# A transformer block with adaptive norms: who rounds the first norm's output, when attention maxima are transposed, and where score blocks stand

## The reference, cut to what matters

```python
c6 = silu(c) @ Wc + bc
sh_msa, sc_msa, g_msa, sh_mlp, sc_mlp, g_mlp = split(c6, 6)
xm = ln(x) * (1 + sc_msa) + sh_msa                     # first norm
q, k, v = xm @ Wq + bq, xm @ Wk + bk, xm @ Wv + bv     # 16 heads of 16 features
w = softmax(q @ k.T / 16)
x = x + g_msa * ((w @ v) @ Wo + bo)
xm2 = ln(x) * (1 + sc_mlp) + sh_mlp                    # second norm
x = x + g_mlp * (gelu(xm2 @ W1 + b1) @ W2 + b2)
```

## Time and profile before

| | before |
|---|---|
| median of 3 runs | 710.11 us (709.73 to 710.66) |
| the profiled execution | 708.81 us |
| its span, first to last instruction | 707.0 us |
| mean granted TensorE clock | 0.992 of full speed |
| busy in the span: TensorE | 670.0 us (95%) |
| VectorE | 552.2 us (78%) |
| ScalarE | 404.6 us (57%) |
| GpSimd | 242.6 us (34%) |

### The profile page before, as it was taken

The page is one execution under the profiler, slowest core; times in us unless marked ns, Lnnn a source line. Parts: engine busy times, 40 slices in busy tenths (PEclk is TensorE's granted clock), DMA queues, the critical chain, the costliest instruction groups (busy, mean ns, idle before and its releaser), DMA issues.

```text
span 707.0 us, 15845 instructions
## 1 busy us (share of the span) xinstructions
PE 670.0 (95%) x6492; PEld 413.5 (58%) x6492; DVE 552.2 (78%) x1019; ACT 404.6 (57%) x485; POOL 242.6 (34%) x179
## 2 busy tenths in 40 slices
PE   7989998889999999999999999999999989999997
PEld 6543345333766448854687448854687436833986
DVE  5988988699977988789867988689867975651673
ACT  7546663576415874288535865278535872388221
POOL 1770015113532036312453036312453122360545
PEclk9999999999999999999999999999999998999999
DMA  8745005410633106330462106230471102021111
GB/s 304 216 105 154 31 32 166 122 62 17 161 97 88 50 32 169 76 120 26 111 154 79 60 32 177 67 121 17 102 172 37 68 36 64 11 83 64 47 31 36
DMA packets 58120, 63.57 MB, mean 90 GB/s; under 512 B 7576, under 2 KB 49070, under 8 KB 58046
## 3 DMA queue, kind: packets, MB, share of 16 engines
q1 hardware_dynamic: 58048, 62.56, 30.7%
HBM read 24.15 MB, written 12.89 MB: 52 GB/s over the span
## 4 chain that ended last, share of the span: by engine, by line
PE 76%; DVE 15%; issue 3%; ACT 3%; POOL 1%; SPq 1%; DMA 1%; ACTq 0%; DVEq 0%; POOLq 0%
PE ps L878 21%; PE ps L824 14%; PE ps L938 13%; PE ps L1014 11%; DVE mx L1285 8%; PE ps L884 6%; PE ps L1093 3%; PE ps L975 2%; PE ps L870 2%; PE ps L1100 1%; PE ps L923 1%; PE ps L983 1%; ACT z L725 1%; ACT prob L759 1%; DVE stats L1205 1%
## 5 line engine op out<-in xcount | busy, mean ns | idle before, releaser
L1285 DVE TENSOR_REDUCE mx<-ps 128x1 f32<-128x512 f32 x512 | 331.1, 684 | 55.2 <-PE ps L884 33.5
L759 ACT ACTIVATE prob<-ps 128x1024 f32<-128x1024 f32 x256 | 249.1, 1022 | 92.4 <-PE ps L878 58.9
L878 PE MATMUL ps<-qst,kst 98*32 98x512 bf16 x1920 | 142.9, 379 | 0.6 <-ACT prob L759 0.6
L938 PE MATMUL ps<-prob,vaug 128*32 128x512 f32 x1024 | 133.7, 594 | 0.7 <-DVE x L1361 0.4
L878 PE MATMUL ps<-kst,qst 96*32 96x512 bf16 x1348 | 128.6, 381 | 5.3 <-DVE mx L1285 4.4
L688 POOL TENSOR_TENSOR hl<-z,hh 128x512 fp32r<-128x512 f32 x63 | 85.1, 1352 | 125.6 <-DVE hh L1500 125.5
L809 ACT ACTIVATE z<-ps,bias_t 128x512 f32<-128x512 f32 x64 | 43.8, 687 | 127.0 <-PE ps L1014 112.2
L878 PEld LDWEIGHTS ps<-qst,kst 98*32 98x32 bf16 x1920 | 52.6, 97 | 67.8 <-issue 27.1
L878 PEld LDWEIGHTS ps<-kst,qst 96*32 96x32 bf16 x1348 | 37.3, 94 | 78.9 <-DVE mx L1285 48.2
L824 PE MATMUL ps<-w_hi,hh 128*128 128x256 f32 x256 | 73.8, 288 | 0.3 <-POOL hl L688 0.3
L824 PE MATMUL ps<-w_lo,hh 128*128 128x256 f32 x256 | 72.2, 282 | 0.0
(11 more groups left out here) (152 smaller groups left out, 937.8 us busy)
## 6 DMA issues: line engine op xcount, KB each, us to landing
qst<-prob SPq DMA_DIRECT2D x72, 128.0 KB, 3.8
kst<-prob SPq DMA_DIRECT2D x72, 128.0 KB, 3.8
y_scratch<-rb SPq DMA_DIRECT2D x28, 256.0 KB, 2.0
xd<-in_x_dram SPq DMA_DIRECT2D x8, 512.0 KB, 4.0
xa<-in_x_dram SPq DMA_DIRECT2D x7, 512.0 KB, 4.6
yc<-y_scratch SPq DMA_DIRECT2D x14, 256.0 KB
rb<-r_scratch SPq DMA_DIRECT2D x14, 256.0 KB
out_dram<-xn SPq DMA_DIRECT2D x7, 512.0 KB, 3.2
```

The lines of the kernel that those rows point to most:

```text
L759: act.activation(prob[:, s % 2, 2 * p:2 * p + 2, :], ps[:, 2 * p:2 * p + 2, :], ACT.Exp, scale=1.0 / DH).then_inc(exp_done, 1)
L878: m = pe.matmul(out[32 * n:32 * n + 32, :], weights[:, 32 * n:32 * n + 32], moving, start=True, stop=True, skip_group_check=True)
L938: m = pe.matmul(ps[32 * q:32 * q + 32, 4 + g % 2, :], vaug[par][:, kt, G * g + q, :], prob[:, s % 2, q, :], start=kt == 0, stop=kt == TT - ...
L1285: dve.tensor_reduce(mx[(i + 1) % 2][:, t, at_column:at_column + 1], ps[:, BANK_OF[q], :], AXX, ALU.max).then_inc(max_done, 1)
```

## The change

It has four parts.

1. `relieved` is now true for the first norm of every batch, so ScalarE writes `zh` from PSUM for batches 3 to 7 too, ahead of z, and VectorE's two casts for each go.
2. `TURN_BEHIND` is one block later for the seven groups of batches 0 and 1. Group (1, 0) comes to the `mid` place of stage 0, and its row copy and its load now stand ahead of batch 2's first parts in the lists of ScalarE and SyncE. Group (0, 0) moves from the last value block of stage -1 to behind the first `down` block, and takes its bank from 6 and 7 in place of 0 and 1.
3. The tables: stage 0's attention has 66 blocks in place of 64 and what follows it 16 in place of 21, with 3 doubled blocks in place of 8. In stage 1 the attention keeps 48, spread in another way, and 37 follow in place of 34. Steady stages keep their numbers, but the blocks between the second MLP products stand at j = 0 to 3 in place of 0 to 4. Blocks of the MLP rotate over banks 6, 7, 0 and 1 from stage 1 on (before over 6, 7 and 1 in stages 1 to 4, and over 6 and 7 in stages 5 and 6).
4. The start of stage 1: inner steps 0 and 1 use two banks in place of one, `wo_products` gets a wait for the maxima up to inner step 1 (bank 7), `y_norm` stands one block later, the residual of batch 0 stands behind inner step 3 in place of 2, and the statistics of its second norm begin at inner step 8 in place of 6.

```diff
@@ -59,15 +59,15 @@


 C_STEADY = ((0,) * STEPS, (1, 1) + (3,) * (STEPS - 4) + (4, 3))
-REST_STEADY = 0, (1, 1), 0, (0, 1, 0, 1), (0, 1, 0, 1), (1, 1, 1), (2, 2, 2, 2, 2, 0, 0, 0)
+REST_STEADY = 0, (1, 1), 0, (0, 1, 0, 1), (0, 1, 0, 1), (1, 1, 1), (3, 3, 2, 2, 0, 0, 0, 0)
 C_FIRST = {
-    0: ((4,) * 9 + (3,) + (0,) * 6, (0,) * 9 + (1,) + (4,) * 6),
-    1: ((2, 1, 1, 2, 3, 3, 3, 3) + (0,) * 8, (0,) * 8 + (4, 3, 4, 3, 4, 4, 4, 4)),
+    0: ((5, 5) + (4,) * 7 + (1,) + (0,) * 6, (0,) * 9 + (3,) + (4,) * 6),
+    1: ((3, 2, 1, 1, 4, 4, 3, 3) + (0,) * 8, (0,) * 8 + (3, 3, 3, 3, 3, 4, 4, 4)),
 }
 REST_FIRST = {
     -1: (2, (4, 0), 3, (0, 2, 0, 2), (1, 1, 1, 1), (), (8,)),
-    0: (0, (1, 1), 3, (0, 2, 0, 2), (1, 1, 1, 1), (), (8,)),
-    1: (0, (1, 1), 0, (0, 1, 0, 1), (0, 1, 0, 1), (3, 3, 3), (4, 4, 4, 4, 3, 0, 0, 0)),
+    0: (0, (2, 2), 3, (0, 2, 0, 0), (1, 1, 1, 1), (), (3,)),
+    1: (0, (1, 1), 0, (0, 1, 0, 1), (0, 1, 0, 1), (3, 3, 3), (6, 6, 5, 5, 0, 0, 0, 0)),
 }


@@ -110,7 +110,7 @@

-TURN_BEHIND = {BLOCKS * b + group_blocks(b, g): (b, g) for b in ROW_ENDS for g in range(row_groups(b))}
+TURN_BEHIND = {BLOCKS * b + group_blocks(b, g) + 1: (b, g) for b in ROW_ENDS for g in range(row_groups(b))}

 SPLIT_BEHIND = {BLOCKS * b + group_blocks(b, g) - 1: (b, g) for b in range(NB) for g in range(row_groups(b))}

@@ -144,7 +144,9 @@
                 n = old[s] + new[s]
                 alone = n if s < 2 or s % TT == 1 else min(n, 2) if s % TT == 2 else 0
                 if i == 1 and s <= WO_FIRST + 1:
-                    blocks(n, (6,), (6,))
+                    blocks(n, (6, 7) if s < WO_FIRST else (6,), (6,))
+                    if s == WO_FIRST - 1:
+                        ahead_of_wo = block
                     continue
                 blocks(alone, (6, 7))
                 blocks(n - alone, (6, 7, 5 - (s - 1) // TT % 2))
@@ -154,16 +156,16 @@
             blocks(ahead, (6, 7, 0, 1), (0, 1))
         else:
             blocks(ahead, (6, 7))
-        blocks(sum(up) + sum(down), (6, 7, 1) if 1 <= i <= 4 else (6, 7))
+        blocks(sum(up) + sum(down), (6, 7, 0, 1) if i > 0 else (6, 7))
         if row_groups(i + 1) == 1:
             take((i + 1, 0), (6, 7))
     assert block == BLOCKS * NB
-    return bank_of, before
+    return bank_of, before, ahead_of_wo

 WO_FIRST, WO_BANKS, WO_FIRST_BANKS = 2, (4, 5), (5, 7)
-BANK_OF, BEFORE = score_banks()
+BANK_OF, BEFORE, AHEAD_OF_WO = score_banks()


 def rows_behind():
@@ -394,7 +396,7 @@

         def relieved(n, b):

-            return n == 0 and (at(b, 0) or at(b, 1) or at(b, 2)) or n == 1 and final(b)
+            return n == 0 or final(b)

         def spared(b):

@@ -543,6 +545,8 @@
                     load_maxima(0, 1)
                     fill_stack(1, 3)
                 elif runs(i, 2):
+                    if i == 0:
+                        load_maxima(1, 0)
                     fill_stack(i + 2, 0, (0,) if i == 0 else (0, 1, 2))
                     if i != 0:
                         fill_stack(i + 2, 1)
@@ -560,7 +564,6 @@
                 if runs(i, 2) and i > 0:
                     fill_stack(i + 2, 2, (1, 2))
                 elif i == 0:
-                    load_maxima(1, 0)
                     fill_stack(i + 2, 1)
                     fill_stack(i + 2, 2)
                 elif i == -2:
@@ -773,6 +776,8 @@
                     modulate(1, i - 1, 0, SH2, SC2)
                 if runs(i, 2):
                     b = i + 2
+                    if i == 0:
+                        maxima_rows(1, 0)
                     for n, j in enumerate(ORDER):
                         act.wait_ge(qk_done, 4 * b + n + 1)
                         if n == 0 and not later(i, 2, 1):
@@ -788,8 +793,6 @@
                         if at(b, 0) and n % 2:
                             act.wait_ge(wmlp_loaded[n // 2], 16)
                             act.activation(w_mlp_high[n // 2], mlp_stage[:, 2048 * (n // 2):2048 * (n // 2 + 1)], ACT.Copy).then_inc(mlp_split, 1)
-                    if i == 0:
-                        maxima_rows(1, 0)
                     for n in range(2):
                         act.wait_ge(v_done, 2 * b + n + 1)
                         act.activation(vaug[par][:, 2 * n:2 * n + 2, :, 0:DH],
@@ -966,6 +969,8 @@

                     amid = b == i and not final(b)
                     pe.wait_ge(yh_done, b + 2 if final(b) else b + 1)
+                    if b == 0:
+                        pe.wait_ge(max_done, AHEAD_OF_WO)
                     for t in range(TT):
                         if t == TT // 2 and amid:
                             first_transposed(i + 1, 1 - par, 0)
@@ -1385,7 +1390,7 @@
                     for g in range(2, NG):
                         last_evacuate(g)

-                ln2 = {6: (0, 1), 7: (2, 3), 8: (4,), 11: (5, 6), 12: (7, 8)} if i == 1 else {3: (0, 1), 4: (2, 3), 5: (4,), 8: (5, 6), 9: (7, 8)}
+                ln2 = {8: (0, 1), 9: (2, 3), 10: (4,), 11: (5, 6), 12: (7, 8)} if i == 1 else {3: (0, 1), 4: (2, 3), 5: (4,), 8: (5, 6), 9: (7, 8)}
                 ln1 = {6: (0, 1), 7: (2, 3), 10: (4,), 13: (5, 6), 14: (7, 8)}
                 for s in range(STEPS):
                     old, new = (n[s] for n in c_blocks(i)) if has_c else (0, 0)
@@ -1394,7 +1399,7 @@
                             row_max(i - 1, 1)
                         elif has_c and n < old + new:
                             row_max(i, 1)
-                        if n == 0 and i == 1 and s == 1:
+                        if n == 1 and i == 1 and s == 1:
                             for part in range(3):
                                 y_norm(0, part)
                         if n < 2:
@@ -1404,7 +1409,7 @@
                             if has_a and later(i, 2, 2):
                                 for k in ln1.get(s, ())[n:n + 1]:
                                     norm_piece(0, i + 2, xa, k)
-                    if i == 1 and s == WO_FIRST:
+                    if i == 1 and s == WO_FIRST + 1:
                         residual(0, WO_FIRST_BANKS)
                 row_max(i, first_blocks)
                 row_max(i, turn_blocks[0])
```

## The result

The changed kernel takes 704.52 us in the median of 6 runs (703.39 to 706.83), the kernel before 709.92 us (708.81 to 711.1). The ratio is 0.9926 with a 95% interval of 0.9908 to 0.9945, so it is faster by 0.74%. The forecast was 699.4 us, with a range of 694.5 to 706.0. The direction and the range held, but the gain is 5.4 us where 10.5 were forecast. The profiled execution took 704.07 us, its span is 702.3 us (before 707.0), and its mean granted clock 0.990.

What follows compares the result with a forecast made beforehand. TensorE was taken to set the pace, so only its stops for other engines pay. Terms -0.6 - 4.5 - 1.5 - 2.2 - 0.6 - 1.35 = -10.75 us gave 698.1 profiled, 699.4 median; range 694.5 to 706.

Steps and rivals of the forecast that it cites:

- inner steps 4 to 15: Stage 1: pieces of two norms spread apart and one block less, 35.2 us to 33.0, -2.2 (bounds 0 and -3).
- the rest of stage 1: Three more MLP blocks cost time, the turn's 0.63 us wait and third-bank stops go: -0.6 us (bounds +1 and -2).
- three signs that the prediction named for being wrong: Wrong if L1093 waits for L742 in steady stages, turn (1, 0) waits over 2 us, or `y_norm` waits for load.
- stage 0's attention: Turns of (0, 2) and (0, 3) gain 0.6 us each, first two inner steps lose 0.6: -0.6 us.
- its end: End of stage 0: earlier split and fewer doubled blocks, transposed scores at 117.85 against 122.97, -4.5 us of this here.
- the start of stage 1: Transposed scores to output product takes 7.0 us instead of 9.0; the turn of (1, 1) waits 0.75, leaving -1.5 us.
- "0" for group (0, 0): Its turn comes 0.6 us later, but VectorE's eight reductions set the end either way: 0 us.
- half of it is given back: Rival, chance 0.22: later parts, longer turn (1, 0), slow clock and late transfers at inner step 6 give 704.1 us.
- Part 2: Steady turn at j == 4 loses its 0.27 us wait for the split, five stages: -1.35 us (bounds 0 and -2).
- Part 1: First norm's high part on ScalarE, stages 1 to 5: 0 for each stage, bounds -0.2 and +0.2 us.
- the two nearly cancel: Steady stage: w = 1 comes 0.1 us earlier, VectorE's low part starts near 422.9 against 422.77.
- a loss of 0.7 us a stage: Stages 1 to 5: if only the durations' difference shows, 3.5 us in all, 702.9 us; chance 0.05.

Runs made afterwards that it cites:

- x12: The kernel before with all turns one block later and nothing else: 711.53 us (ratio 1.0039).
- x2: The changed kernel with eight filler products directly ahead of the turn of group (0, 0): 702.38 us (ratio 0.9894).
- x8: The changed kernel with eight fillers ahead of the turn of (0, 0) and the casts of stages 1 to 5 back on VectorE: 703.20 us.
- x9: The changed kernel with filler products in the three waits at the end of stage 0: 701.85 us (ratio 0.9902).
- x7: The changed kernel with the second norm's pieces of stage 1 at their old places, inner steps 6 to 8, 11 and 12: 705.95 us.
- x6: The changed kernel with the second norm's pieces of stage 1 in inner steps 7 to 11 instead of 8 to 12: 704.40 us.
- x5: The kernel before with only the steady stages' blocks changed, three at two places instead of two at four, over four banks: 707.23 us.
- x3: The kernel before with only ScalarE writing the first norm's high part for all batches: 709.78 us (ratio 1.0005).
- x4: The changed kernel with VectorE making the high part of batches 3 to 7 by casts again: 703.69 us (ratio 0.9918).
- x10: The changed kernel with fillers at turn (0, 0) and the end of stage 0, casts back on VectorE, second norm's pieces one inner step earlier: 699.12 us.
- x1: The changed kernel with group (0, 0) turned at its old place and bank: 704.78 us (ratio 0.9933).

## Why the prediction was half right

Between the profiled execution that the sum gave (698.1 us) and the measured one (704.07) lie 6.0 us. Of these, 1.4 stand ahead of the change, 1.3 at the turn of group (0, 0), 1.4 in inner steps 4 to 15 and 1.1 in the rest of stage 1. The steady stages add 0.4 and the other terms 0.4. Of the three signs that the prediction named for being wrong, two did not appear: the turn of (1, 0) waits 1.22 us, and `y_norm` does not wait for its load. The first did, but without its price: in a steady stage the weight load of w = 1 waits 0.46 us for the evacuation, yet its product starts 4.46 us behind the transposes, where it was 4.63. Two steps failed, a wait priced at nothing and short waits passed over, and three terms were mis-sized.

**Right: stage 0's attention, its end, and the start of stage 1.** The forecasts were -0.6, -4.5 and -1.5 us, and -0.4, -4.4 and -1.4 came. The walk was right in its links too: a split at a fifth of its old time, the first part later against the transposes (8.67 us behind them, before 6.81), and GpSimd's last subtraction as the releaser. In x12, without the tables, the split is slow and the turn waits 2.07 us.

**Wrong: "0" for group (0, 0).** The prediction had the 0.6 us right (it was 0.7) and said that VectorE's reductions set the end either way. They do at full clock, to within 0.3 us (x2). What was missing is that the clock falls at a wait of 2.25 to 2.29 us here (six profiles of six), and half clock makes each block come every 0.85 us instead of 0.61. Together they cost 1.3 us in the profile. The filler is worth 2.1 us in the median of x2 and 0.5 in that of x8. The prediction had read what follows such a wait and charged it to a rival at one place only.

**Wrong: the forecast's silence on the short waits that it created.** It said that TensorE reaches the transposed scores at 116.7 and waits to 117.85. It took this for free, since GpSimd sets the time. In five profiles of seven the clock falls there, with a loss of 2.2 to 3.6 us. Filling the three waits was worth 2.7 us in the median (x9). Before the change one such stretch of 3.4 us stood there (1.7 us lost). So the rival "half of it is given back" had the time right (704.1 against 704.5). Its mechanism was wrong in two of three links: the turn of (1, 0) waited 1.22 us and not 1 us more than the forecast's 1.4, and no load came late to inner step 6. Its third link, the slow clock, was the true one, at other waits.

**Mis-sized: inner steps 4 to 15.** I took -2.2 (35.2 us to 33.0), and -0.8 came. Spreading the norm is worth 0.5 (x7). The waits of TensorE in this stretch went only from 3.5 to 2.6 us, because one piece met GpSimd's addition. A step earlier, the other 1.1 comes too (x6).

**Mis-sized: the steady stages, twice, with opposite signs.** Part 2 was priced at the turn's wait, 0.27 a stage, and gives 0.43 (x5). Where the other 0.16 comes from, no row shows. Part 1 was priced at 0 and costs 0.2 (x3, x4), the outer one of its bounds. The evacuation was walked rightly. What failed is "the two nearly cancel": they cancel for TensorE's w = 1, not for VectorE, whose idle of 0.88 us ahead of the low part cannot be used. The prediction also worked out a loss of 0.7 us a stage from the two durations, by the rule of the Trainium skill ("Perfetto Trace Analysis", section "Optimizing Scalar/DVE Operations"). Its sign was right, its size was too much.

**Mis-sized: the rest of stage 1.** The forecast was -0.6, and +0.5 came. Between the transposes of stages 1 and 2, TensorE's busy time grew from 83.48 to 84.57 us, by 1.1 where I had put 0.7 for three more blocks. Its idle time fell only from 2.64 to 2.07 us, where 1.3 were to go. The windows of the kernel before and of the changed one:

```profile
173.21:259.33 86.12, 83.48 (x827) 52.14 (x823) 75.08 (x141) 48.44 (x59) 28.13 (x21) 1.00 0.31 85
```

```profile
168.87:255.51 86.64, 84.57 (x830) 52.52 (x826) 77.08 (x142) 49.66 (x61) 28.31 (x21) 1.00 0.31 84
```

The turn's wait is gone, as forecast, but waits for VectorE at blocks stay (1.1 us, before 1.8) and one of 0.4 us for GpSimd's low part of the hidden layer is new. This is read from the traces and was not tried alone.

The slow clock goes with much of the difference between runs of one kernel. Runs of the changed kernel at a mean clock of 0.990 take 704.07 and 704.29 us, at 0.992 703.39, and at 0.985 706.83. Runs of the kernel before, beside the experiments, take 710.75 us in the median at 0.990 and 709.58 at 0.992. So the change is worth 6.2 to 6.6 us at an equal clock, and some 1 us of its median gain goes to the clock. The rest of the distance to the forecast is in the mis-sized terms: x10, which repairs two of them and the clock, comes to 699.12 us.

## What to carry to other kernels

A wait of TensorE has a second price, the clock behind it. When an edit leaves TensorE waiting at a place, even where the end is set by another engine, price half speed for what follows as a risk, and try a few useless products in the wait before judging the edit. Look at the granted clock of several executions, since one profile can have luck at the place that decides. And when an edit takes work from an engine, ask what the engine does in the time won: idle in front of its next input, it has won nothing.

## What was not expected of the hardware

Waits far shorter than those that the prediction feared were enough. Three of 0.5, 0.6 and 0.8 us within 3.5 us were: x6's window above, in which they stand and the clock falls (at 118.8 us, inside the third), has TensorE busy 2.11 of 4.00 us. The Trainium skill ("TensorE: Matmul & The Clock Gate", section "A second HAM failure mode: psum-queue depth-cycling") tells of a kernel whose small waits between groups of products let the clock swing. The five of seven profiles agree, and the kernels with fillers, whose products use the same banks in the same order, show that it is the waits and not the banks.

The same wait does not always have the same effect, and a longer one need not have more. At the old place of (0, 0), 2.0 us were followed by half clock in one profile of four, and a single wait of 1.3 us in stage 1 was in x1 and x2. The longest wait of all, 3.12 us in x12, was not: this window around it has TensorE busy 0.68 of 3.80 us and the clock at 1.00 (columns as in the earlier trace rows).

```profile
130.20:134.00 3.80, 0.68 (x12) 0.23 (x4) 3.26 (x6) 1.03 (x2) 0.00 (x0) 1.00 0.63 170
```

What decides between such cases, these runs do not show. The slow stretches lasted 3.4, 6.8 or 13.7 us at the turn of (0, 0), and 6.8 or 10.2 us at the changed end of stage 0.
